# A fused decoder block on one core: the fourth context product is issued directly behind the third

## What is computed

```
x = layernorm(x + ttt_attention(x))            # chunked recurrent attention, 16 heads of 16
x = layernorm(x + cross_attention(x, ctx))     # below
x = layernorm(x + ffn(x))                      # 8-bit quantised activations and weights, silu(gate) * up

# cross attention, 16 heads of 128
q, k, v = x @ Wq, ctx @ Wk, ctx @ Wv
q, k    = rmsnorm(q) * gq, rmsnorm(k) * gk
attn    = softmax(q k^T / sqrt(128))
out     = concat_h(attn_h @ v_h) @ Wo
```

## Time and profile before

| | |
|---|---|
| Median of 3 runs | 466.35 us |
| Lowest, highest | 463.65, 470.18 us |
| Span of the profiled execution, first to last instruction | 463.8 us |
| PE busy in the profiled execution | 373.4 us, 81% |
| DVE, ACT, POOL busy | 274.3, 244.4, 218.3 us |

### The profile page before, as it was taken

One profiled execution on the slowest core, in us unless ns is written; L12 is line 12 of the kernel. 1 busy time (PEld: TensorE's weight loads), 2 busy tenths in 40 slices (PEclk: granted clock), 3 DMA queues, 4 the chain that ended last, 5 costly groups with the idle time before them and its releaser, 6 DMA issues.

```text
span 463.8 us, 11063 instructions
## 1 busy us (share of the span) xinstructions
PE 373.4 (81%) x4570; PEld 231.0 (50%) x4570; DVE 274.3 (59%) x438; ACT 244.4 (53%) x818; POOL 218.3 (47%) x231
## 2 busy tenths in 40 slices
PE   2999967775775764648869999999999999997952
PEld 2445736444544432424536657485665748464531
DVE  1479953898798895362232427474572737446455
ACT  3036942644453567453655484857568484763320
POOL 2044898699699699761303333232334322224001
PEclk9899975977789979777989999999999999998675
DMA  8990000000000000420000000000000000000000
GB/s 265 193 349 28 0 4 4 6 3 4 3 4 3 3 1 2 171 103 0 2 0 1 0 2 2 11 1 12 2 0 13 1 12 1 11 2 0 13 0 23
DMA packets 12625, 14.54 MB, mean 31 GB/s; under 512 B 2192, under 2 KB 11808, under 8 KB 12064
## 3 DMA queue, kind: packets, MB, share of 16 engines
q1 hardware_dynamic: 12544, 13.83, 9.9%
q10 hardware_dynamic: 32, 0.02, 0.0%
HBM read 12.80 MB, written 1.05 MB: 30 GB/s over the span
## 4 chain that ended last, share of the span: by engine, by line
PE 41%; ACT 6%; DVE 5%; POOL 4%; issue 1%; POOLq 0%; ACTq 0%; DVEq 0%
PE ps L566 12%; PE ps L618 11%; PE ps L610 5%; PE ps L598 3%; PE ps L580 3%; PE ps L637 2%; PE ps L589 2%; PE ps L661 1%; ACT qt L881 1%; PE ps L655 1%; POOL kraw L1365 1%; ACT qjunk L871 1%; POOL krs L1364 1%; ACT cxp L902 1%; PE ps L647 1%
## 5 line engine op out<-in xcount | busy, mean ns | idle before, releaser
L566 PE MATMUL ps<-xwq,x1t 128*128 128x512 f32 x128 | 64.5, 634 | 0.9 <-ACT x1t L893 0.9
L816 ACT ACTIVATE junk<-ps 128x128 bf16<-128x128 f32 x128 | 33.9, 292 | 50.9 <-PE ps L479 50.7
L618 PE MATMUL ps<-mvo,cxp 128*128 128x256 f32 x256 | 58.8, 384 | 0.1
L618 PEld LDWEIGHTS ps<-mvo,cxp 128*128 128x128 f32 x256 | 47.9, 191 | 7.2 <-issue 0.7
L479 PE MATMUL ps<-xwk,ctxt 128*128 128x512 f32 x64 | 46.4, 823 | 0.0
L871 ACT ACTIVATE qjunk<-ps 128x128 f32<-128x128 f32 x128 | 33.4, 279 | 17.9 <-PE ps L566 17.7
L487 PEld LDWEIGHTS ps<-ident,kraw 128*128 128x128 f32 x128 | 18.8, 170 | 46.9 <-issue 23.3
L487 PE MATMUL ps<-ident,kraw 128*128 128x128 f32 x128 | 24.6, 326 | 20.3 <-POOL kraw L1365 9.6
L1365 POOL TENSOR_TENSOR kraw<-kraw,krs 128x512 f32<-128x512 f32 x32 | 36.0, 1126 | 2.5
L1364 POOL TENSOR_TENSOR krs<-krs,mhalf 128x4 f32<-128x4 f32 x32 | 35.5, 1110 | 2.7
L566 PEld LDWEIGHTS ps<-xwq,x1t 128*128 128x128 f32 x128 | 23.2, 198 | 26.6 <-issue 24.0
(11 more groups left out here) (214 smaller groups left out, 849.0 us busy)
## 6 DMA issues: line engine op xcount, KB each, us to landing
xn<-in_x_dram SPq DMA_DIRECT2D x4, 512.0 KB, 4.4
xwo<-in_L_xattn_Wo_dram SPq DMA_DIRECT2D x1, 2048.0 KB, 14.9
xwq<-in_L_xattn_Wq_dram SPq DMA_DIRECT2D x1, 2048.0 KB, 9.2
w1n<-in_L_ffn_w_gate_up_dram SPq DMA_DIRECT2D x1, 1408.0 KB, 9.0
ctx<-in_ctx_dram SPq DMA_DIRECT2D x2, 512.0 KB, 9.2
xwv<-in_L_xattn_Wv_dram SPq DMA_DIRECT2D x1, 1024.0 KB, 12.2
xwk<-in_L_xattn_Wk_dram SPq DMA_DIRECT2D x1, 1024.0 KB, 17.0
out_dram<-x SPq DMA_DIRECT2D x8, 128.0 KB, 1.7
```

What stands on the lines that cost most here:

```text
L566: last = mm(bank(n % 2), x1t[:, (i % 2) * D + k * P:(i % 2) * D + (k + 1) * P], xwq[:, k * XH * XD + qn * BANK:k * XH * XD + (qn + 1) * BA ...
L618: last = mm(bank(6 + turn_of[("y", i, 0)] % 2, D), cxp[:, h * P:(h + 1) * P], mvo[:, h * D:(h + 1) * D], start=h == 0, stop=h == XH - 1)
L816: A(junk[:, t * P:(t + 1) * P], bank(bk, P, t * P), ACT.Square, accum_out=kss[:, h:h + 1])
```

## The change

On PE, `context_sum(i - 1, 3)` moves from behind the transposes of query quarter 2 and of `xqt` to directly behind `context_sum(i - 1, 2)`. On ACT, `context_out(i - 1, 3)` moves in the same way ahead of the two `tp_out`. The lists `turns` and `tps`, and with them every wait, stay as they are, since the order within each list does not change.

```
@@ block.tensor @@
                 if prev:
                     context_sum(i - 1, 2)
+                    context_sum(i - 1, 3)
                 if cur:
                     q_transpose(i, 2)
                 if last2:
                     x_transpose_q(i - 2)
-                if prev:
-                    context_sum(i - 1, 3)
                 if last2:
                     gate_up(i - 2, range(0, 2))
@@ block.scalar @@
                 if prev:
                     context_out(i - 1, 2)
+                    context_out(i - 1, 3)
                 if cur:
                     tp_out("qt", i, 2)
                 if last2:
                     tp_out("xqt", i - 2)
-                if prev:
-                    context_out(i - 1, 3)
                 if cur:
                     tp_out("qt", i, 3)
```

## The result

The changed kernel took 466.77 us in the median of its runs, the kernel before 464.35 us in the median of all its runs that stood beside them. The two medians are 2.4 us apart, a ratio of 1.0052. The ratio that this document uses, here and for every experiment, leaves out the runs that are over 1.5% longer than the fastest run of their kernel, and it is 1.0081, with a 95% interval of 1.0047 to 1.0114, so by it the change costs 2.2 to 5.3 us. The same comparison made again at the end of this study gave 1.0034 (0.9989 to 1.0080), so a small loss is likely and its size is not well known. The profiled execution has a span of 467.1 us against 463.8.

What follows compares the result with a forecast made beforehand. The prediction took PE's order of work to bound the main loop. Its terms, 1.6 + 1.0 + 2.4 - 0.5 + 0.4 = +4.9 us, added to 466.35 gave 471.3 us, range 466.0 to 475.5.

Steps and rivals of the forecast that it cites:

- Pairing: Context products 2 and 3 on PE overlap, in part in passes 2 to 5: 1.70 us for both instead of 2.14.
- Passes 2 to 5: Gate/up 0 starts 0.63 us later, 0.24 comes back before the scores: 0.39 us longer each, +1.6 us in all.
- ACT is where it is lost: Passes 2 to 5: PE's saving of 0.44 us is lost in ACT's copies ahead of gate/up 0, 0.63 us later.
- Passes 6 and 7, the order: One more ACT copy ahead of the `xqt` copy: gate/up 0 and scores 0.5 us later, +1.0 us for both.
- Passes 6 and 7, the clock: PE's gap of 2.4 us before gate/up 0 is followed by a stretch at clock 0.50: +2.4 us for both passes.
- if the clock does not fall in 6 and 7: A sign that the forecast is wrong: no stretch at 0.50 after the 2.4 us wait of gate/up 0 in these passes.
- Pass 1: No `xqt` or gate/up there, so the scores start at 250.45 instead of 250.92: -0.5 us.
- Pass 8: At half clock, the `xqt` copy stands behind product 3's copy, gate/up 0 starts at 432.64 instead of 432.25: +0.4 us.
- the clock stays up: Rival: passes 6 and 7 keep clock 1.00, all else as forecast: +2.5 us, 468.9 us; chance 27%.
- The saving counts in full: Rival: row pairing saves up to 1.06 us in all eight passes, 8.5 us less, 457.9 us; chance 4%.
- No overlap: Rival: the pair of passes 2 to 5 hardly overlaps: +7.3 us, 473.7 us; chance 12%.
- the clock in every pass: Rival: the clock also falls in passes 2 to 5, four more low stretches, +6.8 us, 478.1 us; chance 6%.

Runs made afterwards that it cites:

- PE's order alone: PE issues products 2 and 3 as a pair, ACT keeps its order of before, against the kernel before: 1.0045 (1.0007 to 1.0084).
- the fillers: Two extra PE products in the gaps of passes 6 and 7: on the changed kernel 1.0084; with the change in 6 and 7 only 1.0034, unfilled 1.0077.
- ACT's order alone: ACT copies context 3 early as in the change, PE keeps its order of before, against the kernel before: 1.0256 (1.0212 to 1.0300).
- with `xqt` out of the way: Changed kernel with the xqt transposes and copy moved ahead of the copy work of quarter 3, against the kernel before: 0.9904 (0.9874 to 0.9934).
- the kernel with `wo` behind the pair: Changed kernel with xqt transposes and copy moved ahead, and the wo product moved behind products 2 and 3, against the kernel before: 1.0154 (1.0100 to 1.0207).
- the fastest kernel: Changed kernel with the xqt transposes and copy moved ahead, against the kernel before: 0.9904 (0.9874 to 0.9934), 4.4 us faster.
- The early `xqt` without the pair: Kernel before with only the xqt transposes and copy moved ahead, context products unpaired, against the kernel before: 1.0058 (1.0019 to 1.0098).

## Why the prediction was right, step by step

- **Pairing.** Forecast: product 3 some 0.65 us behind its partner, the transposes 1.70 us behind product 2. Measured 1.71. DVE's release of the bank is what limits it: in passes 6 and 7, without `wo`, the pair takes 1.13 us.
- **Passes 2 to 5.** Forecast +0.39 us each; measured +0.16 in passes 3 to 5 and +0.09 in pass 2. Gate/up 0 came 0.58 later instead of 0.63, and from there to the scores it takes 1.99 us, not the 2.17 borrowed from pass 6. In that pass of before gate/up 1 still followed a late copy of context 3; the pattern was close, but not the one that came. Term: 0.6 us in place of 1.6. The forecast worked out two chains, ACT's queue (gate/up 0 at 301.46) and DVE's release of the bank (301.57), and took the later one; PE's order alone shows that this was right, with the same 3.42 us. Its words "ACT is where it is lost" are wrong for these passes, and right for passes 6 and 7.
- **Passes 6 and 7, the order.** Forecast +0.5 each, measured +0.32, for the same reason: gate/up 0 itself comes 0.48 later (383.67 - 379.48 = 4.19 against 3.71).
- **Passes 6 and 7, the clock.** Forecast 1.2 us a fall and two chances in three: measured 1.19 to 1.30 us, in 4 of 6. I forecast the time with both falls, +2.4; at the frequency seen it is 4/6 x 2 x 1.24 = 1.7 on average, by my working. That it costs the median run this much is not shown: the fillers gave nothing in one comparison (1.0084 against 1.0081) and 0.4% by the ratios, 0.1 us by the medians, in the other, and the end of the kernel can give back as much. By the Trainium skill, "TensorE: Matmul & The Clock Gate", "A second HAM failure mode: psum-queue depth-cycling", short idle times between groups let the clock swing. The traces agree for gaps of 2.36 us, and in ACT's order alone for two of six gaps of 1.54 us; they do not for those of 0.94 us in passes 2 to 5, which passed without a fall in the changed kernel. The recorded sign of being wrong, "if the clock does not fall in 6 and 7", was met by half: in the changed profile it fell in pass 7 alone.
- **Pass 1.** Forecast -0.47, measured from product 2 to the scores: 4.13 us before, 251.32 - 247.66 = 3.66 now, -0.47. In this pair of profiles the pass as a whole is 0.63 us longer (226.61 to 251.32, against 226.84 to 250.92), since product 2 comes 1.1 us later behind the scores of pass 0. That is ahead of every changed instruction: the low stretch of the clock that starts at 236 to 238 us is 7.0 us long in this execution and 3.4 in that of before.
- **Pass 8.** Forecast +0.4. From the first context product to the output product it takes 9.73 us before, and 10.13 in the kernel with pass 8 alone changed (422.45 to 432.58): +0.40.
- **Sum.** With the measured terms 0.6 + 0.6 + 1.7 - 0.5 + 0.4 = 2.8 us, inside the interval of 2.2 to 5.3; forecast 4.9. Of it 1.1 us is the order and 1.7 the clock, and the second is an estimate that the timed runs do not confirm. The time of 471.3 was 4.5 above the median of 466.8: 2.0 from the base, since I took the median of three runs, 466.35, where many runs give 464.35, and 2.5 from the effect, +4.9 against +2.4 between the medians.
- **Luck.** Between the medians the effect is that of the rival "the clock stays up" (+2.5), and 466.8 lies 0.8 us above the lower end of the range of 466.0 to 475.5. The interval of the first comparison holds both the forecast's 4.9 and the rival's 2.5; that of the repeated one ends at +3.7 us. That the time fell inside the range is due in part to the spread that the range took in.
- **Rivals.** "The saving counts in full" decided at gate/up 0 no later than 3.08 us behind product 2. It came at 3.42 in the changed kernel, and with `xqt` out of the way at 296.83 - 294.63 = 2.20: then the gain appears, 4.4 us. The mechanism of that rival was right and only its condition unmet. By the row-group rule of the Trainium skill (same page, Part 3) the pair runs at once. The trace agrees with 1.13 us for four matmuls where both may start together, and the kernel got slower all the same. "No overlap" and "the clock in every pass" fell with the first rows of pass 3.

## What to carry to other kernels

A saving on the busiest engine counts only up to the next wait. Before moving an operation, ask two things of what follows it. What does its own wait now hold up on its engine (here six transposes behind product 3's wait for DVE)? And what does its copy now stand ahead of, in the queue of the engine that evacuates it (here the `xqt` copy in passes 6 and 7)? A run with one half of the move tells them apart. If a local wait swallows the gain, look for an operand with an early input (here `xqt`, whose input DVE had written at 292.1 us, 7.5 us ahead of its transposes) that can leave that queue first. Idle time won on TensorE is not neutral either: collected in one gap, it can cost the clock of the work behind it, though no run here shows that the kernel as a whole pays for it.

## What the runs showed of the hardware

- Two products over 64 partitions each, in different halves of the rows, also overlap when the second starts 0.65 us late: 1.78 us for both, against 1.13 when both may start at once and 1.12 for one alone.
- After a PE gap of 2.36 us the granted clock fell to 0.50 in 4 of 6 cases, for about 3.4 us and some 1.2 us of the pass each. Shorter gaps are not safe: behind the six of 1.54 us in passes 2 to 7 of ACT's order alone it fell twice, and behind the four of 1.89 us in passes 2 to 5 of the kernel with `wo` behind the pair once. The two of 1.89 us in passes 6 and 7 of PE's order alone, those of 1.39 us in the same passes of the fastest kernel, and all of 0.94 us ahead of gate/up 0 passed at 1.00. So the length of the gap alone doesn't tell whether the clock falls.
- The scores of pass 0, ahead of all changed work, begin at 226.84 us before and 226.61 with the change, and between 223.77 and 226.86 in the other profiles. So two kernels can stand 3 us apart before the first changed instruction, and from the scores of pass 7 to the end they take 49.42 to 54.23 us, by where the clock is low. The early `xqt` without the pair, at 1.0058 with no pass that differs by 0.1 us, may be a case of it. A difference of 0.5% here needs profiles segment by segment; the times alone left it open.
